# Casting FFN weights straight from DRAM in small pieces, and loading x in whole rows: a transformer layer on 8 cores

## The chip, the cores and the metric

One Trainium2 chip, 8 cores. Each core runs the same program on its own batch element (a sequence of 2048 tokens of width 1024), and no core talks to another. The metric is device time in microseconds (us) of the slowest core; lower is better.

## The reference

One post-norm layer, `x = LN(x + attention(x))`, then `x = LN(x + ffn(x))`, all float32. Cut to what matters here:

```python
q = x @ Wq.T; kv = x @ Wkv_down.T            # kv: 64 wide, shared by 8 heads
k = kv @ Wk_up.T; v = kv @ Wv_up.T
x = layernorm(x + softmax(q k^T / 16) v @ Wo.T)
h = gelu(x @ W1.T + scale * low_rank_1(x) + b1)     # W1: 4096 x 1024
x = layernorm(x + h @ W2.T + scale * low_rank_2(x, h) + b2)   # W2: 1024 x 4096
```

## The kernel before

The program writes its own order: a small planner (`Plan.op`) appends each instruction to the list of one engine, with the semaphore values it waits for. Every engine then runs its list strictly in that order, so an instruction that waits holds up everything behind it on its engine. A wait whose value the engine has already waited for is not issued again.

**Start (lines 181 to 240).** SyncE (SP) issues the loads: eight pieces of `wkvT`, then x in 32 pieces of 128 rows x 512 columns (`xTs`, 256 KB each, 2 KB of a row at a time), then sixteen pieces of `wku`, then `b1s`, `b2s` and `scls`. TensorE's first matmul (line 230, `kv = x @ Wkv_down.T`) waits for two semaphores: `sXT[tb]`, its quarter of x, and `sP0` at its full count `sP0_all`, in which `wkvT`, `wku`, `b1s`, `b2s` and `scls` are counted. Attention follows (lines 332 to 647).

**FFN (lines 653 to 1130).** The tokens go through in four blocks `tb` of 512. In each block, 32 chunks `hc` of W1 (each 1024 x 128) give the hidden activations, and then 64 chunks `(d, g)` of W2 (each 512 x 128) give the output. Products of float32 precision are made from three bf16 matmuls per tile (hi x hi, hi x lo, lo x hi). So each weight chunk is needed as a bf16 part "hi" and a bf16 remainder "lo".

In block 0 these parts are made, and written to DRAM (`w1sd`, `w2sd`) for blocks 1 to 3, which load them back by SP in ready form. `plan_w1(0, hc)` does, for one chunk of W1:

1. SP: eight 64 KB loads `w1f <- w1p`, released when the subtraction of three chunks earlier is done (lines 740 to 745).
2. GpSimd (POOL): one DMA `whl1 <- w1f`, from SBUF to SBUF, that casts the whole chunk from float32 to bf16: the hi part (line 747). It waits for the loads of step 1, for the matmuls that last read this one of four slots (`w1_free`), and for the stores that last read it (`st1_done`).
3. POOL: `tensor_sub`, lo = float32 - hi (line 754), which waits for the DMA of step 2.
4. ScalarE (ACT), in `plan_w1_store`: sixteen 32 KB stores to `w1sd` (lines 765 and 769), which wait for step 3.

`plan_w2` and `plan_w2_store` do the same for a W2 chunk, with four loads (line 790), one casting DMA (line 796), one half as wide `tensor_sub` (line 803) and eight stores (lines 815 and 819). Since POOL runs in order, its list in block 0 is: cast 0, subtract 0, cast 1, subtract 1, and so on. The casting DMA of a chunk is not issued before the subtraction of the chunk before it has been done.

ACT's list in the W1 part of block 0 is: sixteen stores of chunk hc, then the `Gelu` of chunk hc (line 1012), then the stores of chunk hc + 1. TensorE does 24 matmuls for a W1 chunk (lines 979, 984, 989) and 12 for a W2 chunk (lines 1089, 1094, 1099); POOL runs three chunks ahead of it at most.

Of the kernel before, what the change touches and what calls it, by code (L numbers as in the profile page):

```python
# [87 lines left out]
def build_nc():  # L88
# [3 lines left out]
    xT = nc.dram_tensor("xT", [D, T], F32, kind="ExternalInput").ap()  # L92
# [5 lines left out]
    w1p = nc.dram_tensor("w1p", [HCN, D, 128], F32, kind="ExternalInput").ap()  # L98
    w2p = nc.dram_tensor("w2p", [DC, FF, 128], F32, kind="ExternalInput").ap()
# [29 lines left out]
    def row(off, n):  # L129
# [22 lines left out]
    xTs = es_p12.enter_context(nc.sbuf_tensor("xTs", [128, DC * T], F32, side="right"))  # L152
# [11 lines left out]
                 "sW20", "sW21", "sU4", "sT1", "sM",  # L164
                 "sW1C0", "sW1C1", "sW2C0", "sW2C1", "sZ1", "sZT0", "sZT1",
                 "sST0", "sST1", "sST2", "sST3", "sSU0", "sSU1", "sSU2", "sSU3",
                 "sXTa", "sXTb", "sXTc", "sXTd",
                 "sW12", "sW13", "sW22", "sW23"]
    sems = {n: Chan(es.enter_context(nc.semaphore(n))) for n in sem_names}
    with nc.Block() as block:  # L170
        cT, cV, cS, cG = sems["cT"], sems["cV"], sems["cS"], sems["cG"]
        dO = sems["dO"]
        sP0, sBT, sU8, sUA = sems["sP0"], sems["sBT"], sems["sU8"], sems["sUA"]
        sXT = [sems["sXTa"], sems["sXTb"], sems["sXTc"], sems["sXTd"]]
        sU4, sT1, sM = sems["sU4"], sems["sT1"], sems["sM"]
        sWST = [sems["sWST0"], sems["sWST1"]]
        sXQ = [sems["sXQ0"], sems["sXQ1"]]
# [2 lines left out]
        sW1 = [sems["sW10"], sems["sW11"], sems["sW12"], sems["sW13"]]  # L180
        sW2 = [sems["sW20"], sems["sW21"], sems["sW22"], sems["sW23"]]
        P = Plan(block, {"tensor": cT, "vector": cV, "scalar": cS})

        for c in range(DC):
            P.op("sync", lambda e, c=c: e.dma_start(
                out=wkvTs[:, c * LR:(c + 1) * LR],
                in_=wkvT[c * 128:(c + 1) * 128, :]), inc=sP0, inc_k=16)
        dS_wkvT = sP0.n
        dS_xTtb = {}
        for tb in range(NQB):  # L190
            for c in range(DC):
                P.op("sync", lambda e, c=c, tb=tb: e.dma_start(
                    out=xTs[:, c * T + tb * QBS: c * T + (tb + 1) * QBS],
                    in_=xT[c * 128:(c + 1) * 128, tb * QBS:(tb + 1) * QBS]),
                    inc=sXT[tb], inc_k=16)
            dS_xTtb[tb] = sXT[tb].n
        for fc in range(16):
            P.op("sync", lambda e, fc=fc: e.dma_start(
                out=wkus[:, fc * LR:(fc + 1) * LR],
                in_=wku[fc * 128:(fc + 1) * 128, :]), inc=sP0, inc_k=16)  # L200
# [5 lines left out]
        sP0_all = sP0.n  # L206
# [4 lines left out]
            out=idn[:], in_=idn[:], compare_op=ALU.not_equal, fill=1.0,  # L211
            base=0, pattern=[[-1, 128]], channel_multiplier=1),
            waits=[(cG, cG_ms)], inc=cG)
# [14 lines left out]
        for tb in range(NQB):  # L228
            for c in range(DC):
                P.op("tensor", lambda e, tb=tb, c=c: e.matmul(  # L230
                    psA[tb % 2][0:64, :],
                    wkvTs[:, c * LR:(c + 1) * LR],
                    xTs[:, c * T + tb * QBS: c * T + (tb + 1) * QBS],
                    start=(c == 0), stop=(c == DC - 1)),
                    waits=[(sP0, sP0_all), (sXT[tb], dS_xTtb[tb]), cV],
                    inc=(cT if c == DC - 1 else None))
            P.op("vector", lambda e, tb=tb: e.tensor_copy(
                kv[:, tb * QBS:(tb + 1) * QBS], psA[tb % 2][0:64, :]),
                waits=[cT], inc=cV)
# [15 lines left out]
        for kc in range(KC):  # L255
# [3 lines left out]
                waits=[(cG, cG_idn), (cV, cV_kv), cV, cT], inc=cT)  # L259
            P.op("vector", lambda e, kc=kc: e.tensor_copy(  # L260
                kvtok[:, kc * 65:kc * 65 + 64], psA[kc % 2][:, 0:64]),
                waits=[cT], inc=cV)
# [33 lines left out]
        cV_A = cV.n  # L296
# [42 lines left out]
        for p in range(4):  # L339
            for qi in range(NQB):  # L340
                for c in range(DC):
                    P.op("tensor", lambda e, p=p, qi=qi, c=c: e.matmul(  # L342
                        psA[(p * NQB + qi) % 2][:],
                        Asb[:, c * 512 + p * 128: c * 512 + (p + 1) * 128],
                        xTs[:, c * T + qi * QBS: c * T + (qi + 1) * QBS],
                        start=(c == 0), stop=(c == DC - 1)),
                        waits=[(cV, cV_A), (sXT[qi], dS_xTtb[qi]), cV],
                        inc=(cT if c == DC - 1 else None))
                par2 = (p * NQB + qi) % 2
                P.op("vector", lambda e, par2=par2: e.tensor_copy(  # L350
                    qtf[:], psA[par2][:]), waits=[cT, (sBT, dS_BT_done2)], inc=cV)
                cV_qt = cV.n
                P.op("vector", lambda e, p=p, qi=qi: e.tensor_copy(
                    qth_t[:, p * T + qi * QBS: p * T + (qi + 1) * QBS],
                    qtf[:]), inc=cV)
                P.op("vector", lambda e, p=p, qi=qi: e.tensor_sub(
                    qtl_t[:, p * T + qi * QBS: p * T + (qi + 1) * QBS],
                    qtf[:],
                    qth_t[:, p * T + qi * QBS: p * T + (qi + 1) * QBS]), inc=cV)
                P.op("vector", lambda e: e.tensor_mul(  # L360
                    sqp2[:], qtf[:], qtf[:]),
                    waits=[(cT, cT_pairsum)], inc=cV)
                P.op("tensor", lambda e: e.matmul(
                    psU0[0:2, :], onespair[:], sqp2[:], start=True, stop=True),
                    waits=[cV], inc=cT)
# [362 lines left out]
        def plan_w1(tb, hc):  # L728
            s = hc % 3
            s4 = hc % 4  # L730
            if tb > 0:
                for c in range(DC):
                    P.op("sync", lambda e, hc=hc, c=c, s4=s4: e.dma_start(
                        out=whl1[:, s4 * 2048 + c * 256: s4 * 2048 + (c + 1) * 256],
                        in_=w1sd[hc, c * 128:(c + 1) * 128, :]),
                        waits=[(cT, w1_free[s4]), (sST[s4], sST_tot[0][s4])],
                        inc=sW1[s4], inc_k=16)
                dS_w1[(tb, hc)] = sW1[s4].n
                return
            for c in range(DC):  # L740
                P.op("sync", lambda e, hc=hc, c=c, s=s: e.dma_start(
                    out=w1f[:, s * DC * 128 + c * 128: s * DC * 128 + (c + 1) * 128],
                    in_=w1p[hc, c * 128:(c + 1) * 128, :]),
                    waits=[(cG, cG_w1.get((tb * HCN + hc) - 3, 0))],
                    inc=sW1[s], inc_k=16)
            dS_w1[(tb, hc)] = sW1[s].n
            P.op("gpsimd", lambda e, s=s, s4=s4: e.dma_start(
                out=whl1[:, s4 * 2048: s4 * 2048 + 1024],
                in_=w1f[:, s * DC * 128:(s + 1) * DC * 128]),
                waits=[(sW1[s], dS_w1[(tb, hc)]), (cT, w1_free[s4]),  # L750
                       (sST[s4], st1_done.get(s4, 0))],
                inc=sW1C[s % 2], inc_k=16)
            dS_w1c[(tb, hc)] = sW1C[s % 2].n
            P.op("gpsimd", lambda e, s=s, s4=s4: e.tensor_sub(  # L754
                whl1[:, s4 * 2048 + 1024: s4 * 2048 + 2048],
                w1f[:, s * DC * 128:(s + 1) * DC * 128],
                whl1[:, s4 * 2048: s4 * 2048 + 1024]),
                waits=[(sW1C[s % 2], dS_w1c[(tb, hc)]), (cT, w1_free[s4])], inc=cG)
            cG_w1[tb * HCN + hc] = cG.n

        def plan_w1_store(hc):
# [14 lines left out]
        def plan_w2(tb, d, g):  # L776
# [12 lines left out]
            for k in range(4):  # L789
# [3 lines left out]
                    waits=[(cG, cG_w2.get((tb * 64 + d * 8 + g) - 3, 0))],  # L793
                    inc=sW2[s], inc_k=16)
            dS_w2[(tb, d, g)] = sW2[s].n
            P.op("gpsimd", lambda e, s=s, s4=s4: e.dma_start(
                out=whl2[:, s4 * 1024: s4 * 1024 + 512],
                in_=w2f[:, s * 512:(s + 1) * 512]),
                waits=[(sW2[s], dS_w2[(tb, d, g)]), (cT, w2_free[s4]),
                       (sSU[s4], st2_done.get(s4, 0))],  # L800
                inc=sW2C[s % 2], inc_k=16)
            dS_w2c[(tb, d, g)] = sW2C[s % 2].n
            P.op("gpsimd", lambda e, s=s, s4=s4: e.tensor_sub(  # L803
                whl2[:, s4 * 1024 + 512: s4 * 1024 + 1024],
                w2f[:, s * 512:(s + 1) * 512],
                whl2[:, s4 * 1024: s4 * 1024 + 512]),
                waits=[(sW2C[s % 2], dS_w2c[(tb, d, g)]), (cT, w2_free[s4])], inc=cG)
            cG_w2[tb * 64 + d * 8 + g] = cG.n

        def plan_w2_store(d, g):  # L810
# [367 lines left out]
```

How the kernel before makes its waits and increments, by code:

```python
            def body(e, lst=lst, hw=hw):  # L73
                for fn, ws, inc, k in lst:
                    for c, v in ws:
                        if hw.get(id(c), 0) >= v:
                            continue
                        e.wait_ge(c.h, v)
                        hw[id(c)] = v
                    inst = fn(e)
                    if inc is not None:
                        inst.then_inc(inc.h, k)
```

## Time and profile before

| | |
|---|---|
| median of 2 runs | 3872.85 us (3871.45 to 3874.26) |
| profiled execution | 3861.26 us |
| its span on the slowest core (core 1) | 3859.7 us (cores: 3834.9 to 3859.7) |
| TensorE busy | 3040.9 us (79% of the span) |
| VectorE busy | 741.3 us (19%) |
| ScalarE busy | 506.1 us (13%) |
| GpSimd busy | 254.1 us (7%) |
| moved by DMA | 253.88 MB, 66 GB/s on average |

"Busy" is the time in which an engine computes; the issuing of DMAs by SP and ACT isn't counted in it. The shares are averages over the whole span. The kernel is a sequence of stages with different limits: the loads at the start end at 42 us, attention at about 1740 us, block 0 of the FFN at 2460 us, and blocks 1 to 3 fill the rest. POOL's work lies almost wholly in block 0.

### The profile page before, as it was taken

How to read it: one execution, taken by the hardware profiler on the slowest of the kernel's cores; microseconds unless marked ns; L12 is line 12 of the kernel's file. 1: busy time of each engine (PE TensorE's matmuls, PEld its weight loads, DVE VectorE, ACT ScalarE, POOL GpSimd, SP SyncE). 2: the span in 40 equal slices, each digit the busy share in tenths (PEclk: the TensorE clock that was granted, in tenths of full speed). 3: DMA queues.
4: the chain of work that ended last, by engine and by line, in shares of the span. 5: the costliest groups of instructions: out<-in, count | busy, mean ns of one | idle time of the engine just before them, and what ended most of it. 6: DMA issues, size and time to landing. Idle time of an engine off the chain costs nothing.

```text
span 3859.7 us, 32426 instructions; the slowest of 8 cores (3834.9 to 3859.7 us)
## 1 busy us (share of the span) xinstructions
PE 3040.9 (79%) x10610; PEld 1182.7 (31%) x10610; DVE 741.3 (19%) x1123; ACT 506.1 (13%) x729; POOL 254.1 (7%) x312
## 2 busy tenths in 40 slices
PE   3646759969969969952666666689996899879996
PEld 1512223323323323310222222233442344324442
DVE  1112221112112112122222000133102430133101
ACT  0000004414414414400000000011000110011000
POOL 0000000000000000000322233100000000000000
PEclk9578879989989989985888899889998999989998
DMA  4130010001001001002765466523232324423232
GB/s 117 66 109 6 0 27 5 6 7 43 6 4 46 6 4 45 6 18 68 152 136 126 92 143 142 121 78 86 70 96 71 99 69 93 94 66 86 63 98 61
DMA packets 491493, 253.88 MB, mean 66 GB/s; under 512 B 192626, under 2 KB 462962, under 8 KB 491330
## 3 DMA queue, kind: packets, MB, share of 16 engines
q1 hardware_dynamic: 319394, 177.63, 17.6%
q10 hardware_dynamic: 152064, 42.01, 4.8%
q0 software_dynamic: 19872, 32.18, 3.9%
q8 instruction: 88, 1.44, 0.2%
q14 instruction: 75, 0.61, 0.1%
HBM read 177.49 MB, written 50.33 MB: 59 GB/s over the span
## 4 chain that ended last, share of the span: by engine, by line
PE 67%; DVE 9%; DMA 7%; ACTq 6%; issue 6%; ACT 3%; SPq 1%; POOL 0%; DVEq 0%; POOLq 0%
PE psU L597 12%; DMA whl<-w2f 5%; PE ps L342 4%; PE psY L629 3%; ACTq L769 3%; PE ps L563 3%; ACTq L765 3%; PE ps L570 3%; PE ps L567 3%; PE psY L979 2%; PE psY L984 2%; PE psY L989 2%; PE ps L1089 2%; PE ps L1099 2%; PE ps L1094 2%
## 5 line engine op out<-in xcount | busy, mean ns | idle before, releaser
L597 PE MATMUL psU<-et,kvtok 128*65 128x512 f32 x1024 | 523.1, 598 | 2.3
L583 ACT ACTIVATE et<-ps,Ubias 128x512 f32<-128x512 f32 x512 | 351.9, 687 | 643.8 <-PE psU L597 431.6
L1012 ACT ACTIVATE hgf<-htmp,b1s 128x512 f32<-128x512 f32 x128 | 92.4, 722 | 1529.4 <-DVE htmp L1006 1291.5
L1089 PE MATMUL psY<-hphi,whl 128*128 128x512 bf16 x512 | 197.4, 386 | 52.4 <-POOL whl L803 51.5
L1089 PE MATMUL ps<-hphi,whl 128*128 128x512 bf16 x512 | 198.5, 388 | 46.5 <-POOL whl L803 44.6
L979 PE MATMUL psY<-z1s,whl 128*128 128x512 bf16 x512 | 208.9, 408 | 19.5 <-DVE u_bc L964 14.2
L448 DVE RECIPROCAL rcp<-psU 1x512 f32<-1x512 f32 x32 | 107.4, 3355 | 573.3 <-PE psU L597 573.3
L979 PE MATMUL ps<-z1s,whl 128*128 128x512 bf16 x512 | 198.6, 388 | 17.8 <-POOL whl L754 17.8
L984 PE MATMUL psY<-z1s,whl 128*128 128x512 bf16 x512 | 208.5, 407 | 0.0
L989 PE MATMUL psY<-z1s,whl 128*128 128x512 bf16 x512 | 207.1, 405 | 0.0
L1099 PE MATMUL ps<-hphi,whl 128*128 128x512 bf16 x512 | 198.3, 387 | 0.0
L1094 PE MATMUL ps<-hplo,whl 128*128 128x512 bf16 x512 | 198.2, 387 | 0.0
L984 PE MATMUL ps<-z1s,whl 128*128 128x512 bf16 x512 | 198.0, 387 | 0.0
L989 PE MATMUL ps<-z1s,whl 128*128 128x512 bf16 x512 | 197.9, 386 | 0.0
L1099 PE MATMUL psY<-hphi,whl 128*128 128x512 bf16 x512 | 197.2, 385 | 0.0
L1094 PE MATMUL psY<-hplo,whl 128*128 128x512 bf16 x512 | 197.2, 385 | 0.0
L597 PEld LDWEIGHTS psU<-et,kvtok 128*65 128x65 f32 x1024 | 139.8, 139 | 138.2 <-issue 51.9
L629 PE MATMUL psY<-u_all,BT 128*128 128x512 f32 x256 | 128.6, 649 | 45.3 <-DVE xqb L636 26.7
L342 PE MATMUL ps<-xTs,Asb 128*128 128x512 f32 x256 | 144.3, 727 | 18.1 <-DVE qpm L369 17.7
L958 PE MATMUL psL<-rows,ones1r 1*128 1x512 f32 x32 | 25.1, 873 | 121.1 <-DVE hplo L1023 106.4
L563 PE MATMUL ps<-qth_t,kvAh 128*128 128x512 bf16 x256 | 99.5, 389 | 23.2 <-DMA kvBl<-kvAl 18.1
L1019 DVE CAST hphi<-hgf 128x512 bf16<-128x512 f32 x128 | 57.0, 445 | 286.7 <-ACT hgf L1012 286.7
(172 smaller groups left out, 3060.7 us busy)
## 6 DMA issues: line engine op xcount, KB each, us to landing
whl<-w1sd SPq DMA_DIRECT2D x768, 64.0 KB, 2.1
whl<-w2sd SPq DMA_DIRECT2D x768, 64.0 KB, 2.1
w1f<-w1p SPq DMA_DIRECT2D x256, 64.0 KB, 2.4
w1sd<-whl ACTq DMA_DIRECT2D x512, 32.0 KB, 2.0
w2f<-w2p SPq DMA_DIRECT2D x256, 64.0 KB, 2.9
w2sd<-whl ACTq DMA_DIRECT2D x512, 32.0 KB, 2.5
xTs<-xT SPq DMA_DIRECT2D x32, 256.0 KB, 9.3
wst<-wq SPq DMA_DIRECT2D x16, 512.0 KB, 4.4
```

The lines of the kernel that those rows point to most:

```text
L342: P.op("tensor", lambda e, p=p, qi=qi, c=c: e.matmul(psA[(p * NQB + qi) % 2][:], Asb[:, c * 512 + p * 128: c * 512 + (p + 1) * 128], xTs[: ...
L563: P.op("tensor", lambda e, kc=kc, par=par, kvh=kvh, qs=qs: e.matmul(psA[par][:], kvh[:, kc * 128:(kc + 1) * 128], qth_t[:, qs:qs + QBS], s ...
L567: P.op("tensor", lambda e, kc=kc, par=par, kvh=kvh, qs=qs: e.matmul(psA[par][:], kvh[:, kc * 128:(kc + 1) * 128], qtl_t[:, qs:qs + QBS], s ...
L583: P.op("scalar", lambda e, kc=kc, par=par, h=h: e.activation(out=et[:, par * 512:(par + 1) * 512], in_=psA[par][:], func=AF.Exp, bias=Ubia ...
L597: P.op("tensor", lambda e, kc=kc, par=par, h=h: e.matmul(psU[h % 2][:], kvtok[:, kc * 65:(kc + 1) * 65], et[:, par * 512:(par + 1) * 512], ...
L629: P.op("tensor", lambda e, d=d, lc=lc: e.matmul(psY[d % 2][:], BT[:, lc * D + d * 128: lc * D + (d + 1) * 128], u_all[:, lc * 512:(lc + 1) ...
L979: P.op("tensor", lambda e, c=c, s4=s4, hi1=hi1: e.matmul(psP[s4][:], whl1[:, hi1: hi1 + 128], z1s[:, c * 512:(c + 1) * 512], start=(c == 0 ...
L984: P.op("tensor", lambda e, c=c, s4=s4, hi1=hi1: e.matmul(psP[s4][:], whl1[:, hi1: hi1 + 128], z1s[:, 4096 + c * 512: 4096 + (c + 1) * 512] ...
L989: P.op("tensor", lambda e, c=c, s4=s4, lo1=lo1: e.matmul(psP[s4][:], whl1[:, lo1: lo1 + 128], z1s[:, c * 512:(c + 1) * 512], start=False, ...
L1089: P.op("tensor", lambda e, d=d, hi2=hi2, hc=hc, st=st: e.matmul(psP[d % 4][:], whl2[:, hi2: hi2 + 128], hphi[:, hc * 512:(hc + 1) * 512], ...
L1094: P.op("tensor", lambda e, d=d, hi2=hi2, hc=hc: e.matmul(psP[d % 4][:], whl2[:, hi2: hi2 + 128], hplo[:, hc * 512:(hc + 1) * 512], start=F ...
L1099: P.op("tensor", lambda e, d=d, lo2=lo2, hc=hc, k=k: e.matmul(psP[d % 4][:], whl2[:, lo2: lo2 + 128], hphi[:, hc * 512:(hc + 1) * 512], st ...
```

## The change

Two edits, in three places.

- The loads of x: eight DMAs of whole rows (128 rows x 2048 columns, 1 MB each) instead of 32, issued ahead of `wkvT` instead of behind it, all counted on `sP0`. The four semaphores of x go.
- The casting DMA of `plan_w1` in block 0: eight DMAs, each a 128 x 128 piece, that read float32 directly from `w1p` in DRAM and write bf16 into `whl1`, instead of one from `w1f`. They no longer wait for the loads of `w1f`; the `tensor_sub` waits for these now. The loads of `w1f` stay.
- The same in `plan_w2`: four DMAs from `w2p` instead of one from `w2f`.

```diff
         for c in range(DC):
             P.op("sync", lambda e, c=c: e.dma_start(
+                out=xTs[:, c * T:(c + 1) * T], in_=xT[c * 128:(c + 1) * 128, :]),
+                inc=sP0, inc_k=16)
+        dS_xT = sP0.n
+        for c in range(DC):
+            P.op("sync", lambda e, c=c: e.dma_start(
                 out=wkvTs[:, c * LR:(c + 1) * LR],
                 in_=wkvT[c * 128:(c + 1) * 128, :]), inc=sP0, inc_k=16)
         dS_wkvT = sP0.n
-        dS_xTtb = {}
-        for tb in range(NQB):
-            for c in range(DC):
-                P.op("sync", lambda e, c=c, tb=tb: e.dma_start(
-                    out=xTs[:, c * T + tb * QBS: c * T + (tb + 1) * QBS],
-                    in_=xT[c * 128:(c + 1) * 128, tb * QBS:(tb + 1) * QBS]),
-                    inc=sXT[tb], inc_k=16)
-            dS_xTtb[tb] = sXT[tb].n
...
-            P.op("gpsimd", lambda e, s=s, s4=s4: e.dma_start(
-                out=whl1[:, s4 * 2048: s4 * 2048 + 1024],
-                in_=w1f[:, s * DC * 128:(s + 1) * DC * 128]),
-                waits=[(sW1[s], dS_w1[(tb, hc)]), (cT, w1_free[s4]),
-                       (sST[s4], st1_done.get(s4, 0))],
-                inc=sW1C[s % 2], inc_k=16)
+            for c in range(DC):
+                P.op("gpsimd", lambda e, hc=hc, c=c, s4=s4: e.dma_start(
+                    out=whl1[:, s4 * 2048 + c * 128: s4 * 2048 + (c + 1) * 128],
+                    in_=w1p[hc, c * 128:(c + 1) * 128, :]),
+                    waits=[(cT, w1_free[s4]), (sST[s4], st1_done.get(s4, 0))],
+                    inc=sW1C[s % 2], inc_k=16)
...
-                waits=[(sW1C[s % 2], dS_w1c[(tb, hc)]), (cT, w1_free[s4])], inc=cG)
+                waits=[(sW1C[s % 2], dS_w1c[(tb, hc)]),
+                       (sW1[s], dS_w1[(tb, hc)]), (cT, w1_free[s4])], inc=cG)
...
-            P.op("gpsimd", lambda e, s=s, s4=s4: e.dma_start(
-                out=whl2[:, s4 * 1024: s4 * 1024 + 512],
-                in_=w2f[:, s * 512:(s + 1) * 512]),
-                waits=[(sW2[s], dS_w2[(tb, d, g)]), (cT, w2_free[s4]),
-                       (sSU[s4], st2_done.get(s4, 0))],
-                inc=sW2C[s % 2], inc_k=16)
+            for k in range(4):
+                P.op("gpsimd", lambda e, d=d, g=g, k=k, s4=s4: e.dma_start(
+                    out=whl2[:, s4 * 1024 + k * 128: s4 * 1024 + (k + 1) * 128],
+                    in_=w2p[d, (g * 4 + k) * 128:(g * 4 + k + 1) * 128, :]),
+                    waits=[(cT, w2_free[s4]), (sSU[s4], st2_done.get(s4, 0))],
+                    inc=sW2C[s % 2], inc_k=16)
...
-                waits=[(sW2C[s % 2], dS_w2c[(tb, d, g)]), (cT, w2_free[s4])], inc=cG)
+                waits=[(sW2C[s % 2], dS_w2c[(tb, d, g)]),
+                       (sW2[s], dS_w2[(tb, d, g)]), (cT, w2_free[s4])], inc=cG)
```

## Rows read from the trace of the kernel before

**Rows 1.** The page: the chain that ended last, shares of the span by line.
```profile
PE psU L597 12%; DMA whl<-w2f 5%; PE ps L342 4%; PE psY L629 3%; ACTq L769 3%; PE ps L563 3%; ACTq L765 3%; PE ps L570 3%; PE ps L567 3%; PE psY L979 2%; PE psY L984 2%; PE psY L989 2%; PE ps L1089 2%; PE ps L1099 2%; PE ps L1094 2%
```
**Rows 2.** Busy time by stretch: W1, then W2, of block 0.
```profile
core 1: us, PE busy (x) PEld busy (x) DVE busy (x) ACT busy (x) POOL busy (x), PEclk, DMA share, GB/s
1828.00:2160.00 332.00, 218.02 (x872) 88.72 (x872) 67.21 (x104) 24.37 (x33) 85.94 (x65) 0.81 0.58 125
2160.00:2460.00 300.00, 201.54 (x782) 77.42 (x782) 5.59 (x8) 0.00 (x0) 109.56 (x132) 0.92 0.66 138
```
**Rows 3.** Waits, W2 stretch (2160 to 2460): total us, times, longest.
```profile
POOL whl L803 <- DMA whl<-w2f: 185.4, 64, 4.4
PE psY L1089 <- POOL whl L803: 51.5, 26, 7.7
PE ps L1089 <- POOL whl L803: 44.6, 26, 3.3
```
**Rows 4.** One line, L796 (W2 cast): ns min/median/max, first to last start; landing.
```profile
L796 POOL DMA_DIRECT2D whl<-w2f x64: 573/573/583, 2163.4 to 2453.5; - x64
DMA to landing us min/median/max: 2.3/3.2/4.9
```
**Rows 5.** Timeline of POOL, start of W2: start us, us [idle before].
```profile
2161.95 1.51 POOL L1059 DMA_DIRECT2D r<-r  x3 [0.49 <-issue]
2163.45 0.57 POOL L796 DMA_DIRECT2D whl<-w2f  x1
2165.93 1.15 POOL L803 TENSOR_TENSOR whl<-w2f,whl 128x512 bf16<-128x512 f32 x1 [1.91 <-DMA whl<-w2f]
2167.03 0.58 POOL L796 DMA_DIRECT2D whl<-w2f  x1
```
**Rows 6.** The page: DMA issues, KB each, median us from issue to landing.
```profile
w1f<-w1p SPq DMA_DIRECT2D x256, 64.0 KB, 2.4
w2f<-w2p SPq DMA_DIRECT2D x256, 64.0 KB, 2.9
```
**Rows 7.** Waits, W1 stretch (1828 to 2118).
```profile
POOL whl L747 <- DMA w1sd<-whl: 85.8, 24, 6.6
```
**Rows 8.** Lines L747 (landing of the W1 cast), L765, L1012 in the W1 stretch.
```profile
DMA to landing us min/median/max: 2.9/3.7/5.7
L765 ACTq DMA_DIRECT2D w1sd<-whl x256: 326/451/1136, 1833.3 to 2142.6; - x128
L1012 ACT ACTIVATE hgf<-htmp,b1s x32: 721/722/723, 1843.5 to 2143.6; 128x512 f32<-128x512 f32 x32
```
**Rows 9.** Timeline of POOL, first and last chunk of W1.
```profile
1828.02 0.57 POOL L747 DMA_DIRECT2D whl<-w1f  x1
1831.09 2.12 POOL L754 TENSOR_TENSOR whl<-w1f,whl 128x1024 bf16<-128x1024 f32 x1 [2.50 <-DMA whl<-w1f]
1833.16 0.57 POOL L747 DMA_DIRECT2D whl<-w1f  x1
...
2112.84 2.11 POOL L754 TENSOR_TENSOR whl<-w1f,whl 128x1024 bf16<-128x1024 f32 x1 [2.64 <-DMA whl<-w1f]
```
**Rows 10.** DMA queues in the W2 stretch (2163 to 2459): packets, MB, share.
```profile
q10 hardware_dynamic: 72720, 16.58, 26.5%
q1 hardware_dynamic: 35136, 16.01, 22.4%
q0 software_dynamic: 9311, 8.42, 17.5%
```
**Rows 11.** The start: waits until 120 us, and busy time in stretches as in rows 2.
```profile
PE ps L230 <- DMA scls<-scl: 42.1, 1, 42.1
...
10.00:15.00 5.00, 0.00 (x0) 0.00 (x0) 0.00 (x0) 0.00 (x0) 0.00 (x0) 1.00 0.95 265
25.00:30.00 5.00, 0.00 (x0) 0.00 (x0) 0.00 (x0) 0.00 (x0) 0.00 (x0) 1.00 1.04 312
```
**Rows 12.** DMA issues again: a small POOL DMA to 128 partitions.
```profile
sqf<-rows POOLq DMA_DIRECT2D x8, 2.0 KB, 1.9
```

More of the change, by code:

```diff
@@ L166, in build_nc @@
                  "sST0", "sST1", "sST2", "sST3", "sSU0", "sSU1", "sSU2", "sSU3",
-                 "sXTa", "sXTb", "sXTc", "sXTd",
                  "sW12", "sW13", "sW22", "sW23"]
@@ L173, in build_nc @@
         sP0, sBT, sU8, sUA = sems["sP0"], sems["sBT"], sems["sU8"], sems["sUA"]
-        sXT = [sems["sXTa"], sems["sXTb"], sems["sXTc"], sems["sXTd"]]
         sU4, sT1, sM = sems["sU4"], sems["sT1"], sems["sM"]
@@ L234, in build_nc @@
                     start=(c == 0), stop=(c == DC - 1)),
-                    waits=[(sP0, sP0_all), (sXT[tb], dS_xTtb[tb]), cV],
+                    waits=[(sP0, sP0_all), cV],
                     inc=(cT if c == DC - 1 else None))
@@ L346, in build_nc @@
                         start=(c == 0), stop=(c == DC - 1)),
-                        waits=[(cV, cV_A), (sXT[qi], dS_xTtb[qi]), cV],
+                        waits=[(cV, cV_A), cV],
                         inc=(cT if c == DC - 1 else None))
```

## Prediction

> **What bounds the kernel now.** I read the page first, then the stretches of FFN block 0, the only place where the two casting DMAs run, and inside them the waits and POOL's timeline.
>
> The page's chain [rows 1] gives 5% of the span to one DMA, `whl<-w2f`: the W2 cast. No other DMA stands as high. So the chain runs through POOL's DMAs in the W2 stretch.
>
> In that stretch TensorE is busy 201.5 of 300 us [rows 2]. The waits [rows 3] show why it isn't more: POOL waits 185.4 us in 64 pieces for its own casting DMA, 2.9 us a chunk, and TensorE waits 51.5 + 44.6 = 96 us for POOL's subtraction. The cast starts run from 2163.4 to 2453.5 [rows 4], 63 steps: 4.60 us a chunk. Its anatomy is in the timeline [rows 5] and the landing [rows 4]: 3.2 us from issue to landing, 0.13 us until the subtraction starts, and 1.10 us from there to the next cast's issue; that is 4.43, and the mean over 64, larger than the median's, makes it 4.60. TensorE's part is 12 matmuls at some 0.2 us, under 3 us. **W2 of block 0 is a serial loop on POOL: issue, landing, subtraction, next issue.**
>
> W1 of block 0 is different. There POOL spends most waits on the stores of the slot it wants to overwrite: 85.8 us in 24 pieces [rows 7]. ACT issues 16 stores at 0.45 us and more (7.2 us, in practice near 8) and a Gelu of 0.72 us per chunk [rows 8], and its Gelus run from 1843.5 to 2143.6, 31 steps of 9.68 us. POOL's own cycle, seen at the first chunk before any store can hold it, is 1833.16 - 1828.02 = 5.14 us [rows 9], and with the median landing of 3.7 us [rows 8] 3.7 + 0.13 + 2.07 = 5.9. So ACT's queue of stores sets W1's pace, and POOL is ahead: its last subtraction starts at 2112.84 [rows 9], the last Gelu at 2143.6.
>
> At the start, the first matmul waits until 42.1 us for the last little load, `scls` [rows 11], which stands behind x in SP's queue. The DMA engines are 95% to over 100% busy at 265 to 312 GB/s meanwhile [rows 11].
>
> **The change part by part.**
>
> *W2 casts.* Removed: the wait of the cast for `w2f`, which costs nothing now (loads land in 2.9 us [rows 6] and are issued three chunks ahead, 14 us). Nothing in the waits of the stretch names it. It only moves to the subtraction. The serial loop stays: POOL runs in order, and cast n+1 is still listed behind subtraction n. Added: three more DMA issues per chunk in this loop. One issue with the cast takes 0.573 us [rows 4], three without a cast back to back took 1.51 us together, 0.50 each [rows 5]; so three more cost 1.51 to 1.72, and I take 1.72, the row with the cast. What changes in return is the landing of the last piece. It moves a quarter of the bytes (64 KB read), but from DRAM. Below: a POOL DMA to 128 partitions with next to no bytes takes 1.9 us [rows 12]. Above: the present cast's 3.2 under the same load [rows 4]. The nearest row is the same 64 KB from the same tensor in the same stretch by SP: 2.9 us [rows 6]. I take 2.9. New cycle: 1.72 + 2.9 + 0.13 + 1.10 = 5.85 us against 4.60, so +1.25 us x 64 = **+80 us**. The bounds of it: 1.51 + 1.9 + 1.23 = 4.64, +3 us; and 1.72 + 4.9 (the longest landing of rows 4) + 1.23 = 7.85, +208 us, if every landing were like the worst.
>
> Does the DMA load rise much? The shares in the stretch of 296 us x 16 engines = 4736 us give [rows 10]: casts 17.5% = 829 us; SP's loads 22.4% = 1061 us for 35136 packets of mostly 512 B, 30 ns each; ACT's stores 26.5% = 1255 us for 72720 packets of mostly 256 B, 17 ns each. The new casts are 64 x 512 = 32768 rows of 512 B read and 256 B written; at 30 ns that is 983 us, 154 more over a longer stretch. So the share falls, and landings should not grow for that reason.
>
> The 17 ns of a 256 B row are this kernel's measure of small writes. The Trainium skill (DMA: Bandwidth & Descriptors, Specifications) says that below 512 B the DMA does a read-modify-write; the old cast wrote 1 KB rows, the new one writes 256 B, so by that rule the new pieces carry a penalty. The trace's 256 B stores show none beside the 512 B loads. If each row cost 60 ns instead of 30, the casts would take 1966 us, 1.9 us per chunk on each engine, and the landing would move from 2.9 towards 3.5: about +40 us more. It counts in the dear case below.
>
> *W1 casts.* Seven more issues of 0.573 us, 4.0 us. The last piece's landing: bounds 1.9 [rows 12] and 3.7 [rows 8], nearest row 2.4 (64 KB of `w1p` by SP [rows 6]); I take 2.7, since the cast rows are dearer than SP's. POOL's cycle becomes 4.0 + 2.7 + 0.13 + 2.07 = 8.9 us, from 5.9. The cover is ACT's pace of 9.68. POOL's lag behind ACT at the end is also free: POOL-bound, the last Gelu would start at 1828.0 + 32 P + 8.5 (its 16 stores and a gap), which is 2143.6 for P = 9.6. With P = 8.9 the cover holds. What remains is the first chunk: its subtraction ends 3.8 us later and everything behind it shifts: **+4 us**. If the cover is gone (P = 9.9 with the 3.7 landing) it is +10; nothing speaks for a gain, because ACT's issuing isn't touched. Queued behind POOL's issues there are only the next subtraction and later casts; `u4` and `r2` copies stand ahead of the W1 and W2 runs.
>
> *x in whole rows.* SP's issues shrink from 59 to 35 and x starts 3.7 us earlier (eight `wkvT` issues of 0.47 stood in front: issue of x at 4.8, of the first load at 1.07). But the stretch to 42 us is DMA-bound, and the bytes stay: 8.4 MB of x and 0.8 MB in small rows. At the best rate seen, 312 GB/s, x takes 27 us; at the 265 of [rows 11], 32 us. Then the 24 small-row loads follow. From 2.5 us: 2.5 + 27 to 32 + 4 + 2.1 for the last landing = 36 to 41 instead of 42. I take 37: **-5 us**, bounds -8 and +1. All that follows is a chain from this matmul on, so it arrives at the end in full. The waits of line 342 on x were long satisfied: nothing.
>
> *Sum.* 80 + 4 - 5 = +79 us on the profiled 3859.7 (its run 3861.3), so 3940. The median of the runs lies 0.3% above the profiled run, so 3872.85 + 79 = **3952 us**. Blocks 1 to 3 load ready parts and are not touched.
>
> **Rivals.** What a measurement can tell from no change is 2%: 3795.4 and 3950.3 are the borders.
>
> 1. *Forecast:* W2's loop grows by 0.95 to 1.65 us; with the -1 of the other parts, 3932 to 3977. 0.48.
> 2. *Cheap landing:* the last piece, with few bytes and its siblings ahead of it, lands in 1.9 to 2.6 us. W2 +3 to +61, total 3875 to 3932: no measurable change. For it: the 1.9 of [rows 12]. Against it: that row had an idle DMA system around it, this stretch is 66% busy [rows 2]. 0.20.
> 3. *Dear pieces:* landings of 3.3 to 4.5 us by packets of all three queues interleaving, W2 +106 to +182; POOL becomes W1's bound too, P of 9.6 to 10.8, up to +38. Total 3977 to 4092. For it: landings up to 4.9 exist [rows 4], the slow 256 B rule above. 0.22.
> 4. *Serial pieces:* POOL's DMAs are served one after another at 1 us or more instead of 0.57. Then W2 is 3 x 1.0 + 2.9 + 1.23 = 7.1 (+162) and W1 7 + 2.7 + 2.2 = 11.9 (+74): 4104 and up. Against it: after four POOL DMAs in a row the first W2 cast landed as quickly as its fastest, 2.3 us [rows 4, 5]. 0.06.
> 5. *The other side, not slower but faster than before:* the float32 load was hidden in the loop, and the cast, started without it, is always landed when POOL comes to the subtraction. It decides from a last landing under 1.85 us (1.51 + 1.85 + 1.23 = 4.6). At 1.6, W2 is -16, with x at -8: 3850. It could only be if POOL's order let casts run ahead, which it doesn't. 0.04, with 0.02 for over 2%.
>
> **How the numbers follow.** Likeliest 3952. Range: from inside case 2 (3895) to well into case 3 (4065), leaving about 1 in 10 on each side; it includes both bounds of the landing's likely part. Slower by over 2% (above 3950.3): half of case 1 and all of 3 and 4, 0.24 + 0.22 + 0.06 = 0.52. Faster: 0.02. Within: 0.46.
>
> **What would show it.** In the changed kernel's profile: the W2 stretch of block 0 should last about 375 us instead of 300, with cast groups of four starting 0.57 us apart and 5.85 us between subtractions; POOL's wait for the cast should fall to 2.3 us behind the last issue; TensorE's wait for POOL should grow from 96 to about 175 us. W1's Gelus should still step by some 9.7 us. The first matmul should start near 37 us. The forecast is wrong if the last landing is far from 2.9 us, or if the issues aren't 0.57 us apart.

## The result: slower by 4.2%, and where the 150 us are in the profile after

The ratio of the changed kernel to the one before is **1.0424, 95% interval 1.0406 to 1.0441**, that is +164 us on 3872.85. The profiled executions, one of each kernel, stand at 3861.3 and 4012.4 us (spans 3859.7 and 4010.4, +150.7). The medians over all executions, 3960.27 and 4095.34, include some that other states of the chip had lengthened; the ratio leaves these out.

The page after, its chain's shares by line (compare [rows 1]), and its two new groups of POOL issues (busy us, mean ns):

```profile
PE psU L592 11%; DMA whl<-w2p 5%; PE ps L337 4%; DMA whl<-w1p 3%; PE psY L624 3%; POOL whl L743 3%; PE ps L558 3%; PE ps L565 3%; PE ps L562 3%; POOL whl L793 3%; PE psY L976 2%; PE psY L981 2%; PE psY L986 2%; PE psY L1086 2%; PE ps L1086 2%
...
L793 POOL DMA_DIRECT2D whl<-w2p x256 | 138.8, 561 | 4.3 <-issue 4.2
L743 POOL DMA_DIRECT2D whl<-w1p x256 | 137.2, 574 | 2.2 <-issue 2.2
```

ACT's store issues (L765 and L769, 6% together in rows 1) have left the chain. In their place stand the W1 pieces (3%) and POOL's issuing itself (3% in W1, 3% in W2): W1 has changed its bound from ACT to POOL.

The lines of the casts and subtractions (ns min/median/max, first to last start; the landing belongs to the line above it):

```profile
L743 POOL DMA_DIRECT2D whl<-w1p x256: 527/577/710, 1828.0 to 2156.7; - x128
DMA to landing us min/median/max: 2.2/3.5/5.4
...
L749 POOL TENSOR_TENSOR whl<-w1f,whl x32: 2113/2116/2397, 1835.1 to 2159.6; 128x1024 bf16<-128x1024 f32 x32
...
L793 POOL DMA_DIRECT2D whl<-w2p x256: 527/557/581, 2193.2 to 2601.4; - x128
DMA to landing us min/median/max: 2.1/3.1/4.5
...
L799 POOL TENSOR_TENSOR whl<-w2f,whl x64: 1146/1146/1147, 2197.1 to 2604.9; 128x512 bf16<-128x512 f32 x64
```

| core 1, profiled | before | after | difference |
|---|---|---|---|
| start to first W1 cast | 1828.0 us | 1828.0 | 0 |
| first W1 cast to first W2 cast | 335.4 | 365.2 | **+29.8** |
| first W2 cast to last subtraction | 292.7 | 411.7 | **+119.0** |
| from there to the end (blocks 1 to 3) | 1403.6 | 1405.5 | +1.9 |
| step between W1 subtractions | 9.09 | 10.47 | +1.38 |
| step between W2 subtractions | 4.61 | 6.47 | +1.86 |

So nearly all of the loss lies in block 0, four fifths of it in W2. One W2 chunk in the chain of the changed kernel (start us, us, what), first the part of three issues, then the last piece's landing:

```profile
2352.95 1.60 POOL whl L793 x3
2354.55 3.30 DMA whl<-w2p
...
2359.16 1.60 POOL whl L793 x3
2360.76 3.72 DMA whl<-w2p
```

This is the loop of [rows 5], with 1.60 us of issues put in and a landing that did not get shorter: 3.30 and 3.72 for 64 KB, where one DMA of four times the bytes took 3.2 [rows 4].

### The profile page after: what moved, and what is told of

Its sections match the earlier page's. It is cut to its first block, busy times and chain, and to the rows that moved or that the text cites. A ratio compares the mean times of both kernels' runs of the same rounds, so it can differ in the third digit from the quotient of the medians.

```text
span 4010.4 us, 32814 instructions; the slowest of 8 cores (3992.1 to 4010.4 us)
## 1 busy us (share of the span) xinstructions
PE 3123.2 (78%) x10610; PEld 1199.2 (30%) x10610; DVE 759.6 (19%) x1123; ACT 506.1 (13%) x729; POOL 474.3 (12%) x728
## 4 chain that ended last, share of the span: by engine, by line
PE 64%; DMA 11%; DVE 8%; issue 7%; POOL 6%; ACT 2%; SPq 1%; DVEq 0%; POOLq 0%; ACTq 0%
PE psU L592 11%; DMA whl<-w2p 5%; PE ps L337 4%; DMA whl<-w1p 3%; PE psY L624 3%; POOL whl L743 3%; PE ps L558 3%; PE ps L565 3%; PE ps L562 3%; POOL whl L793 3%; PE psY L976 2%; PE psY L981 2%; PE psY L986 2%; PE psY L1086 2%; PE ps L1086 2%
## 5 line engine op out<-in xcount | busy, mean ns | idle before, releaser
L1086 PE MATMUL psY<-hphi,whl 128*128 128x512 bf16 x512 | 207.8, 406 | 84.7 <-POOL whl L799 83.8
L1086 PE MATMUL ps<-hphi,whl 128*128 128x512 bf16 x512 | 207.3, 405 | 83.9 <-POOL whl L799 83.1
L976 PE MATMUL psY<-z1s,whl 128*128 128x512 bf16 x512 | 215.3, 420 | 58.5 <-POOL whl L749 44.3
L976 PE MATMUL ps<-z1s,whl 128*128 128x512 bf16 x512 | 206.2, 403 | 52.9 <-POOL whl L749 52.9
L981 PE MATMUL psY<-z1s,whl 128*128 128x512 bf16 x512 | 214.8, 420 | 0.0
L986 PE MATMUL psY<-z1s,whl 128*128 128x512 bf16 x512 | 213.1, 416 | 0.0
L1096 PE MATMUL psY<-hphi,whl 128*128 128x512 bf16 x512 | 208.2, 407 | 0.0
L1091 PE MATMUL psY<-hplo,whl 128*128 128x512 bf16 x512 | 208.0, 406 | 0.0
L1091 PE MATMUL ps<-hplo,whl 128*128 128x512 bf16 x512 | 207.4, 405 | 0.0
L1096 PE MATMUL ps<-hphi,whl 128*128 128x512 bf16 x512 | 206.7, 404 | 0.0
L981 PE MATMUL ps<-z1s,whl 128*128 128x512 bf16 x512 | 204.7, 400 | 0.0
L986 PE MATMUL ps<-z1s,whl 128*128 128x512 bf16 x512 | 204.0, 398 | 0.0
L793 POOL DMA_DIRECT2D whl<-w2p x256 | 138.8, 561 | 4.3 <-issue 4.2
L743 POOL DMA_DIRECT2D whl<-w1p x256 | 137.2, 574 | 2.2 <-issue 2.2
```

Source lines behind the costliest of these rows:

```text
L743: P.op("gpsimd", lambda e, hc=hc, c=c, s4=s4: e.dma_start(out=whl1[:, s4 * 2048 + c * 128: s4 * 2048 + (c + 1) * 128], in_=w1p[hc, c * 128 ...
L793: P.op("gpsimd", lambda e, d=d, g=g, k=k, s4=s4: e.dma_start(out=whl2[:, s4 * 1024 + k * 128: s4 * 1024 + (k + 1) * 128], in_=w2p[d, (g * ...
L976: P.op("tensor", lambda e, c=c, s4=s4, hi1=hi1: e.matmul(psP[s4][:], whl1[:, hi1: hi1 + 128], z1s[:, c * 512:(c + 1) * 512], start=(c == 0 ...
L981: P.op("tensor", lambda e, c=c, s4=s4, hi1=hi1: e.matmul(psP[s4][:], whl1[:, hi1: hi1 + 128], z1s[:, 4096 + c * 512: 4096 + (c + 1) * 512] ...
L986: P.op("tensor", lambda e, c=c, s4=s4, lo1=lo1: e.matmul(psP[s4][:], whl1[:, lo1: lo1 + 128], z1s[:, c * 512:(c + 1) * 512], start=False, ...
L1086: P.op("tensor", lambda e, d=d, hi2=hi2, hc=hc, st=st: e.matmul(psP[d % 4][:], whl2[:, hi2: hi2 + 128], hphi[:, hc * 512:(hc + 1) * 512], ...
```

## The experiments

"W1 step" and "W2 step" are the times between subtractions in block 0, from first to last start on the slowest core. The ratio is to the kernel before on the same chip.

| kernel | W1 step | W2 step | W2 step, all eight cores | ratio (95%) |
|---|---|---|---|---|
| before | 9.09 | 4.61 | 4.31 to 4.61 | 1 |
| changed | 10.47 | 6.47 | 6.42 to 6.69 | 1.0424 (1.0406 to 1.0441) |
| e1: one cast DMA per chunk, from DRAM | 8.88 | 5.64 | 5.50 to 5.64 | none; see text |
| e2: pieces, but from SBUF | 9.86 | 6.20 | 6.10 to 6.25 | 1.0376 (1.0322 to 1.0431) |
| e3: W2 casts alone | 9.12 | 6.23 | 6.23 to 6.56 | 1.0378 (1.0307 to 1.0449) |
| e4: changed, nearly no stores | 9.95 | 5.59 | 5.58 to 5.78 | 1.0235 (1.0178 to 1.0293) |
| e12: changed, nearly no float32 loads | 9.11 | 5.76 | 5.51 to 5.90 | none; see text |
| e6: before, casts issued ahead | 9.03 | 4.07 | 4.00 to 4.09 | 0.9916 (0.9892 to 0.9940) |
| e7: before, stores put together | 6.79 | 4.66 | 4.54 to 4.66 | 0.9763 (0.9742 to 0.9785) |
| e8: x loads alone | 9.13 | 4.68 | 4.25 to 4.68 | 0.9992 (0.9967 to 1.0017) |
| e9: changed, pieces issued ahead | 8.96 | 4.09 | 4.02 to 4.09 | 0.9865 (0.9777 to 0.9953) |
| e10: x loads, ahead, stores together | 6.06 | 3.66 | 3.62 to 3.80 | 0.9580 (0.9460 to 0.9700) |
| e11: e10 with the DRAM pieces | 6.93 | 3.59 | 3.54 to 3.72 | 0.9664 (0.9569 to 0.9758) |

The cores of one execution differ: core 1, the slowest before, also has the longest W2 step before (4.61, median of the eight cores 4.42), so by the medians the change costs 2.11 us per chunk and not 1.86 (4.42 to 6.53). A difference of 0.3 us between two kernels says something only where the ranges of the eight cores lie apart.

**Is it the number of pieces or their source?** e1 casts a chunk in one DMA from DRAM (the W2 part; W1 likewise):

```diff
...
-            for k in range(4):
-                P.op("gpsimd", lambda e, d=d, g=g, k=k, s4=s4: e.dma_start(
-                    out=whl2[:, s4 * 1024 + k * 128: s4 * 1024 + (k + 1) * 128],
-                    in_=w2p[d, (g * 4 + k) * 128:(g * 4 + k + 1) * 128, :]),
+            P.op("gpsimd", lambda e, d=d, g=g, s4=s4: e.dma_start(
+                out=whl2[:, s4 * 1024: s4 * 1024 + 512].rearrange(
+                    "p (k f) -> p k f", f=128),
+                in_=w2p[d, g * 512:(g + 1) * 512, :].rearrange(
+                    "(k p) f -> p k f", p=128)),
...
```

> The changed kernel, but each chunk's cast is one DMA again, still from DRAM: the same 1024 (W1) or 512 (W2) rows of 512 B in one issue. Theory A, the count of POOL DMAs costs (their issues, and each queues behind the one before): the W2 cycle of block 0 falls from 6.47 us to about 4.7 (0.57 issue, 3.0 to 3.4 landing, 1.23), W1 is again set by ACT's stores, ratio to the kernel before 0.995 to 1.005. Theory B, the source in DRAM and the small rows cost: the last row lands as late as now, some 5.1 us after the first issue, W2 cycle 6.3 us, ratio 1.035 to 1.045.

Measured: neither. The two executions that can be compared took 3917.6 and 3950.7 us, where the kernel before took 3843.9 to 3871.3, so some 2% are lost; two are too few for an interval. W2's step is 5.64 us, in the middle. The cast's line in W2:

```profile
L792 POOL DMA_DIRECT2D whl<-w2p x64: 780/780/808, 2187.5 to 2542.0; - x64
DMA to landing us min/median/max: 3.3/4.3/4.9
```

Against [rows 4]: the issue has grown from 0.573 to 0.780 us, because the same bytes now come as 512 rows and not 128, and the landing from 3.2 to 4.3. Small rows, read from DRAM, cost 1.03 us per chunk without any further DMA. In W1 the step (8.88) is no longer than before (9.09).

e2 keeps the pieces and reads them from SBUF (`in_=w2f[:, s * 512 + k * 128: s * 512 + (k + 1) * 128]`, and the same for W1; the pieces wait for the float32 loads again).

> The changed kernel, with the same 8 or 4 pieces per chunk, but read from w1f or w2f in SBUF as before. Theory A (count of DMAs): nothing gained, W2 cycle 6.2 to 6.5 us, W1 cycle near 10.3, ratio 1.037 to 1.045. Theory B (DRAM source): only the issues remain, the last landing falls from 3.5 to about 2.5 us, W2 cycle 5.4 us, W1 below ACT's 9.7, ratio 1.010 to 1.018.

Measured: 1.0376 and 6.20 us in W2, 9.86 in W1. **Cutting the cast in pieces explains most of it: +1.59 of the +1.86 us in W2; the DRAM source adds 0.27** (0.38 by the medians of the cores, whose ranges lie apart). In W1 the source weighs more: 9.09 before, 9.86 with pieces from SBUF, 10.47 from DRAM. The interval of e2 just touches that of the changed kernel. "In pieces" still holds two things, three more issues and four times as many rows; e1 shows that rows and source alone make 1.03 of the 1.86, and no run has the issues without the rows.

e3 changes the W2 casts alone (the loads of x and the W1 casts as before).

> The kernel before with the W2 casts alone changed (4 pieces from DRAM), W1 casts and the loads of x as before. If the parts add up: W2 takes 119 us more as in the changed kernel, ratio 1.029 to 1.033, and the W1 stretch is as before. If the W1 casts and their backlog matter for W2, it is less than 1.025.

Measured: 1.0378 with an interval of 1.0307 to 1.0449, above the 1.029 to 1.033 that was expected, though the interval reaches into it. The W2 step is 6.23 against the 6.47 with everything changed, but on the eight cores 6.23 to 6.56 against 6.42 to 6.69, which overlap. The parts roughly add, but this run can't tell whether W1's change costs 0.5% more.

**Why does a quarter of the bytes land no earlier?** First, one burst alone. e5 is the kernel before with test DMAs of POOL during attention, where few others run.

> The kernel before with test DMAs of POOL in query blocks 1 to 3 of attention, where nearly no other DMA runs, each group waited for before the next, its data unused: eight 128 x 128 casting pieces from DRAM; eight such from SBUF; one 128 x 1024 cast from SBUF; one 1024-row cast from DRAM. Theory A (POOL's pieces are served one after another, slower than they are issued, whatever else runs): the landing grows from piece to piece by 0.2 us or more also here, 2.1 us for the first to 3.5 or more for the eighth. Theory C (the growth comes from the loads and stores beside them): every piece lands 2.0 to 2.3 us after its issue, the eighth too; one cast of 1024 rows from DRAM in under 4 us.

The four kinds, in this order: eight pieces from DRAM, eight from SBUF, one 128 x 1024 cast from SBUF, the same from DRAM in 1024 rows (ns min/median/max of the issue; landing):

```profile
L561 POOL DMA_DIRECT2D qdst<-w1p x24: 561/576/612, 918.2 to 1502.3; - x24
DMA to landing us min/median/max: 2.1/2.4/3.1
...
L567 POOL DMA_DIRECT2D qdst<-qsrc x24: 548/564/590, 944.1 to 1528.2; - x24
DMA to landing us min/median/max: 1.8/1.8/2.2
...
L572 POOL DMA_DIRECT2D qdst<-qsrc x3: 555/555/555, 970.0 to 1550.4; - x3
DMA to landing us min/median/max: 3.2/3.2/3.2
...
L575 POOL DMA_DIRECT2D qdst<-w1p x3: 913/918/931, 995.9 to 1576.4; - x3
DMA to landing us min/median/max: 4.2/4.4/4.5
```

The queueing of POOL's pieces behind one another (theory A) is thereby out as the main cause: issued 0.53 us apart, the pieces from SBUF land in 1.8 us, the eighth too; from DRAM the first seven land after 2.1 to 2.5 us at the median, the fourth after 2.2, and the eighth after 3.0 (on the seven other cores after 2.1 to 2.5). The forecast of under 4 us for 1024 rows from DRAM was a little low (4.4). In the loaded W2 stretch of the changed kernel the four pieces of a burst land after some 2.7, 3.0, 3.2 and 3.5 us. So most of what makes them late is beside them. It isn't the subtraction's new wait for the float32 loads: those of its chunk had landed at least 12 us before each W2 subtraction.

e4 takes away ACT's stores (all but those of the first four chunks; the later blocks load these four again):

```diff
-                if tb == 0:
+                if tb == 0 and hc < 4:
                     plan_w1_store(hc)
...
-                    if tb == 0:
+                    if tb == 0 and d == 0 and g < 4:
                         plan_w2_store(d, g)
```

> The changed kernel with ACT's stores of the split weights left out for all but the first four chunks of W1 and of W2 (blocks 1 to 3 load those four again and again, so the output is not the reference's). Theory C, the pieces land late because ACT's stores share the DMA engines: without them the last piece lands 2.3 to 2.6 us after its issue, W2 cycle 5.2 to 5.5 us, W1 cycle 8.3 to 8.8, ratio to the kernel before 0.99 to 1.01. Theory A (POOL's pieces queue behind one another whatever else runs): last landing stays at 3.2 to 3.5 in W2, cycle 6.2 to 6.5, W1 10 or more, ratio 1.035 to 1.045.

Measured: the W2 step falls to 5.59 us, near what theory C said, and the pieces land in 2.4 us at the median. The ratio, 1.0235, lies between the two theories. W1's step on the slowest core, 2, is 9.95, and 9.97 on core 3, but on the six others it is 8.95 to 9.09, from 10.02 to 10.54 in the changed kernel. Here the subtractions of core 0, 31 steps of 9.09 us:

```profile
L749 POOL TENSOR_TENSOR whl<-w1f,whl x32: 2113/2117/2122, 1827.8 to 2109.5; 128x1024 bf16<-128x1024 f32 x32
```

So the stores delayed the pieces in W1 too, though theory C's 8.3 to 8.8 was too low; why cores 2 and 3 stayed behind is open. e12 takes away SP's float32 loads instead (all but those of the first three chunks):

> The changed kernel with SP's float32 loads of w1f and w2f left out for all but the first three chunks of each (the later subtractions use those again, so the lo parts are not the reference's); the DRAM pieces and ACT's stores stay. If the pieces land late because everything that one subtraction releases (pieces, loads, stores) shares the DMA engines, the last piece lands earlier here too, as it did without the stores: W2 cycle 5.7 to 6.1 us instead of 6.47, W1 9.1 to 9.7 instead of 10.47, ratio 1.015 to 1.030. If only the stores disturb the pieces: W2 6.3 to 6.5, W1 10.2 to 10.5, ratio 1.037 or more.

Measured: W2 5.76, W1 9.11, both as the first theory had it; the one execution that can be compared took 3942 us, against 3848.6 to 3872.8 of the kernel before. Two consecutive chunks of W2 on POOL, in the changed kernel and in e12 (the bracket is POOL's idle time before the subtraction):

```profile
2359.16 2.17 POOL L793 DMA_DIRECT2D whl<-w2p  x4
2364.68 1.15 POOL L799 TENSOR_TENSOR whl<-w2f,whl 128x512 bf16<-128x512 f32 x1 [3.35 <-DMA whl<-w2p]
2365.78 2.17 POOL L793 DMA_DIRECT2D whl<-w2p  x4
2371.82 1.15 POOL L799 TENSOR_TENSOR whl<-w2f,whl 128x512 bf16<-128x512 f32 x1 [3.87 <-DMA whl<-w2p]
```

```profile
2299.55 2.17 POOL L793 DMA_DIRECT2D whl<-w2p  x4
2303.83 1.15 POOL L799 TENSOR_TENSOR whl<-w2f,whl 128x512 bf16<-128x512 f32 x1 [2.11 <-DMA whl<-w2p]
2304.94 2.16 POOL L793 DMA_DIRECT2D whl<-w2p  x4
2309.34 1.15 POOL L799 TENSOR_TENSOR whl<-w2f,whl 128x512 bf16<-128x512 f32 x1 [2.24 <-DMA whl<-w2p]
```

Same issues, same subtraction; only the idle time differs. In sum, for a W2 chunk: 1.60 (three issues) + 2.2 (the fourth piece in the quiet of e5) + 0.71 (loads beside it, e12) + 0.88 (stores beside it, e4) + 1.30 (0.20 from the landing to the subtraction, 1.10 from there to the next issue) = 6.7, measured 6.47. So the two parts don't quite add; no run had both out. The Trainium skill (DMA: Bandwidth & Descriptors, Rules for kernel authors) says that DMAs issued from SP, ACT and GpSimd all run on the same 16 DMA engines and interleave. The traces agree: without ACT's stores the last piece of W2 lands 0.9 us sooner (2.6 for 3.5), without SP's loads 0.6 us (2.9).

A likely reason why this strikes so hard is the moment. One subtraction's end releases everything at once: POOL's next pieces, ACT's stores of the chunk just made, and SP's loads into the buffer just freed. In the changed kernel, after the subtraction that started at 2351.84 and took 1.15 us:

```profile
2352.95 2.17 POOL L793 DMA_DIRECT2D whl<-w2p  x4
2353.06 13.18 SPq L786 DMA_DIRECT2D w2f<-w2p  x9
2353.07 0.36 ACTq L812 DMA_DIRECT2D w2sd<-whl  x1
...
2356.37 0.45 ACTq L816 DMA_DIRECT2D w2sd<-whl  x1
2358.05 1.15 POOL L799 TENSOR_TENSOR whl<-w2f,whl 128x512 bf16<-128x512 f32 x1 [2.93 <-DMA whl<-w2p]
```

ACT's eight stores are issued within 3.9 us, all while the pieces are under way. The queues' shares in W2 of the changed kernel (2205 to 2605 us, 6400 us of engine time):

```profile
q0 software_dynamic: 35712, 8.14, 23.2%
q10 hardware_dynamic: 71424, 16.28, 19.9%
q1 hardware_dynamic: 34560, 15.74, 16.7%
```

A row takes 41.6 ns on POOL's queue (0.232 x 6400 / 35712), 31 ns on SP's, 18 on ACT's. One chunk has 32 rows of POOL, 32 of SP and 64 of ACT per DMA engine: 1.33 + 0.99 + 1.15 = 3.5 us of work on each engine, released by one event, while the engines are 60% busy on average. How much of it the last piece really waits for is not shown: no run moved the stores or loads to another moment.

**Is the loop on POOL really what turns late landings into time?** e6 is the kernel before with POOL's order changed: the cast of chunk n + 1 stands ahead of the subtraction of chunk n.

```diff
+            def sub2(s=s, s4=s4, d=d, g=g, gi=gi):
+                P.op("gpsimd", lambda e, s=s, s4=s4: e.tensor_sub(
...
+            if pend2[0] is not None:
+                pend2[0]()
+            pend2[0] = sub2
...
```

> The kernel before, with one change of order: POOL issues the cast of chunk n + 1 ahead of the subtraction of chunk n, for W1 and W2 (the two counting semaphores of the casts alternate by chunk). If the serial loop issue, landing, subtraction on POOL is what bounds W2 of block 0, its cycle falls from 4.6 us to 4.0 or less (the next bound: eight stores of ACT at 0.48, 3.9), and W1, set by ACT's sixteen stores, stays at 9.1: ratio 0.985 to 0.992. If the DMA engines or ACT bound W2 already: no change.

Measured: 0.9916 and a W2 step of 4.07 us, a hair above the 4.0 that was expected, W1 at 9.03. POOL now waits for ACT's stores (105.7 us in W2). e9 does the same to the changed kernel, all its DRAM pieces included:

> The changed kernel (all its DRAM pieces) with POOL's order as in e6: the pieces of chunk n + 1 are issued ahead of the subtraction of chunk n. If the pieces cost time only because POOL waits for the last one in a serial loop, the loss goes: W2 cycle 4.0 to 4.4 us (ACT's stores), W1 9.1 to 9.4, ratio to the kernel before 0.990 to 1.000. If the DMA engines can't carry the pieces beside loads and stores: W2 cycle stays above 5.5, ratio above 1.02.

Measured: **0.9865 (0.9777 to 0.9953), W2 4.09 us**, W1 8.96, a little better than expected. POOL in W2 (start us, us, idle before):

```profile
2306.54 2.17 POOL L803 DMA_DIRECT2D whl<-w2p  x4 [0.25 <-issue]
2308.69 1.21 POOL L810 TENSOR_TENSOR whl<-w2f,whl 128x512 bf16<-128x512 f32 x1
2310.52 2.17 POOL L803 DMA_DIRECT2D whl<-w2p  x4 [0.63 <-DMA w2sd<-whl]
2312.67 1.20 POOL L810 TENSOR_TENSOR whl<-w2f,whl 128x512 bf16<-128x512 f32 x1
```

Next to no idle time is left before the subtractions (3.7 us in all), though the pieces still take 3.0 us to land at the median and the DMA engines are 97% busy (2200 to 2400 us, the three queues):

```profile
q0 software_dynamic: 27854, 6.35, 36.1%
q10 hardware_dynamic: 55852, 12.73, 32.9%
q1 hardware_dynamic: 28056, 12.78, 28.3%
```

The 4% are gone, with the same number of DMAs, bytes and rows, and the W2 step is that of e6 (4.09 and 4.07). So with ACT's stores as they are, the pieces cost time only through the serial order: issue, wait for the landing, subtract, and not before then issue again.

**What covered W1?** e7 leaves POOL's order and puts ACT's stores together, two DMAs per chunk, hi and lo, instead of 16 or 8, with the same rows:

> The kernel before with ACT's stores put together: 2 DMAs for a chunk instead of 16 (W1) or 8 (W2), the same rows and bytes. If ACT's issuing sets W1's pace, the W1 cycle of block 0 falls from 9.1 to POOL's own 5.9 to 6.5 us, about 90 us in all, and W2 stays at 4.4 to 4.7: ratio 0.973 to 0.980. If it is the DMA engines that bound W1, no more than 10 us.

Measured: 0.9763, the W1 step 6.79 us (0.3 above what was expected; 6.28 to 6.42 on six of the eight cores), W2 4.66. ACT's issuing was W1's pace, as the prediction had it, and it was the larger of the two things to gain. e8 is the loads of x alone:

> The kernel before with only the loads of x changed (8 whole-row DMAs ahead of wkvT). By the forecast 5 us less, ratio 0.9985; in the trace of the changed kernel the first matmul came 4.2 us earlier on core 1 and up to 8 on others, and the W1 stretch began at the same time: ratio 0.998 to 1.000.

Measured: 0.9992, interval 0.9967 to 1.0017: nothing that can be told from zero, and at most 0.3%.

**Versions that beat both.** e10 joins the loads of x, e6's order and e7's stores, with the cast from SBUF; e11 has the DRAM pieces instead.

> The casts as before (one DMA from SBUF), e6's order, e7's two stores per chunk, and the whole-row loads of x: W1 cycle 5.9 to 6.3 us (some 5.9 us of DMA engine work per chunk), W2 cycle 3.0 to 3.6 us, ratio 0.950 to 0.962. If the two edits take the same time away and don't add: 0.970 or more.

> As e10, but with the DRAM pieces of the changed kernel instead of the one cast from SBUF. POOL issues 8 x 0.57 + 2.1 = 6.7 us per W1 chunk and 4 x 0.55 + 1.15 = 3.4 us per W2 chunk, and the pieces take 41 to 50 ns a row on the DMA engines: W1 cycle 6.8 to 7.5, W2 3.6 to 4.2, ratio 0.965 to 0.978, slower than e10 by 1 to 2%.

Measured: e10 0.958 (0.946 to 0.970), fastest run 3699.5 us; e11 0.966 (0.957 to 0.976), 3721.5 us. W2's step in e10, 3.66 us, is a little above the range; POOL now waits there for SP's float32 loads. That e10 is ahead of e11 shows in W1 (6.06 against 6.93 us, where POOL's issuing of eight pieces, 8 x 0.57 + 2.1, binds), but the intervals of the ratios overlap, so that e10 is faster by 1% or more, as expected, isn't shown.

## Why the prediction was wrong

The direction and the serial loop of W2 were right; the landing of the last piece was put too short, in W2 and in W1, and with it the size came out at half. That W1 would stay covered by ACT was wrong. +79 us were forecast and 164 measured (150.7 between the profiled executions: W2 119.0 for 80, W1 29.8 for 4, x nothing for -5, the rest 1.9). By the ratio of 1.0424 the time is 4037 us on the base of 3872.85, inside the range's upper part, but the named number 3952 was far off, and that the time still lies in the range owes nothing to the sum. What happened is the third rival, "dear pieces", to which 0.22 was given: it had W2 at +106 to +182 and W1 up to +38, with W1's bound gone over to POOL.

- *The W2 issues:* 1.72 us forecast, 1.60 measured, right. Back to back an issue takes 0.53 us, less than the 0.573 of a single one.
- *The last piece's landing in W2, the term that failed:* 2.9 us forecast, 3.30 and 3.72 in the chain above, 3.48 on average (0.57 of issue, POOL's mean idle time of 199.0 / 64 = 3.11 before the subtraction, less 0.20 from the landing to the subtraction). This is +0.58 x 64 = 37 us. The 0.20 itself was forecast as 0.13; it is 4 us more. The prediction took SP's 64 KB loads [rows 6] as the nearest row. But that is a median over all four loads of a burst, while POOL waits for the last of its burst, and in a burst under load each piece lands later than the one before (2.7, 3.0, 3.2, 3.5 us).
- *"The share falls, and landings should not grow for that reason":* the share fell (0.66 to 0.59), and the reasoning failed nonetheless. An average over the cycle doesn't tell what is under way while the pieces are: e4 and e12 show that stores and loads each add to the landing. The row was also priced at 30 ns, SP's price, and cost 41.6 in POOL's queue. The prediction did weigh a dearer row, 60 ns, by the Trainium skill's rule of a read-modify-write below 512 B (DMA: Bandwidth & Descriptors, Specifications). ACT's stores don't show that rule at work: their rows of 256 B cost 18 ns, less than SP's 512 B rows. Whether the rule has a part in the 41.6 ns of POOL's rows, which are cast and written as 256 B, no run tells.
- *W1: "the cover holds", wrong:* the same term. The last of eight pieces was put at 2.7 us and lands after 4.4 on average (0.57 of issue, POOL's mean idle time of 127.4 / 32 = 3.98, less 0.20); so POOL's cycle is 10.47 and not 8.9 us, above ACT's 9.68 and above the 9.6 that the prediction itself named as the break-even. The cost was 30 us instead of 4. The formula for the end of W1 was sound: 1828.0 + 32 x 10.47 + 8.5 = 2171.5, and the last Gelu started at 2170.7. The W2 casts began 22.5 us after it, against 19.8 before.
- *x:* the first matmul started at 37.9 us, where 37 was forecast, 4.2 us earlier than before. On core 1 nothing of it arrived at W1. The waits until 240 us, before and after, say where it went:

```profile
PE ps L311 <- DMA wst<-woT: 13.3, 1, 13.3
...
PE ps L306 <- DMA wst<-woT: 16.8, 1, 16.8
```

  The matmul behind it waited 3.5 us longer for the loads of `woT`. On the seven other cores that matmul came 2 to 8 us earlier than before, and their first W1 cast 0.4 to 13.6 us earlier. "It arrives at the end in full" was too bold for the slowest core; e8 measures 0.08% less, with an interval that holds both nothing and the forecast's 0.15%.
- *Serial pieces and the faster side* (rivals 4 and 5) didn't come: issues kept 0.53 to 0.57 us apart, and no piece in W2 landed in 1.85 us (2.1 at the least).
- *A small misreading:* TensorE's 12 matmuls took 3.1 us per W2 chunk before (201.5 us for 782 of them, [rows 2]) and not under 3; at 4.60 a step nothing hung on it.

## What to carry to other kernels

When a wait stands in a serial loop of one in-order engine, cutting its transfer in pieces adds all issues but one to the loop and makes the loop wait for the last piece; look first whether the next transfer can be issued ahead of the work that waits for this one, which here was worth more than the whole damage (1.042 to 0.987). Price the landing by the last transfer of a burst, with the transfers that run beside it, and not by a median or an average share. And an engine whose busy time looks small may be bound by issuing DMAs: ACT was 13% busy, and putting its stores together gave 2.4%.

## What the runs showed of the hardware that was not expected

- POOL's issue time depends on the rows: 0.53 to 0.58 us for 128 rows, 0.78 for 512 (e1) and 0.92 for 1024 (e5), with like bytes.
- A row of 512 B costs more on POOL's casting queue (41.6 ns in the changed kernel) than a row of like size on SP's (31 ns). That the cast makes it dearer is not shown.
- The granted clock of TensorE was lower in W2, where TensorE was busy 60% of the stretch instead of 67%: 0.80 after 0.92 [rows 2]:

```profile
2193.00:2607.00 414.00, 248.61 (x772) 86.93 (x773) 5.25 (x7) 0.00 (x0) 209.73 (x321) 0.80 0.59 99
```

  Some 780 matmuls took 248.6 us of busy time instead of 201.5, at both levels of the clock. In one chunk of the changed kernel they start 0.22 us apart at first and 0.43 us apart at its end:

```profile
2360.20 0.38 PE L1091 MATMUL ps<-hplo,whl 128*128 128x512 bf16 x1
2360.42 0.54 PE L1096 MATMUL ps<-hphi,whl 128*128 128x512 bf16 x1
...
2361.18 0.63 PE L1091 MATMUL ps<-hplo,whl 128*128 128x512 bf16 x1
2361.60 0.63 PE L1096 MATMUL ps<-hphi,whl 128*128 128x512 bf16 x1
```

  It cost little there, because 12 matmuls at the lower level (5.1 us) still fit in a step of 6.47; POOL waited only 6.7 us for TensorE in the whole stretch. They would not have fitted in the 4.61 us of the kernel before.
